# Two chained attention layers on one core: score tiles accumulated as key differences, and each unit's work in a new order

## The reference, cut to what matters

```python
h = group_norm(x)                        # 32 groups, 2 channels each
q, k, v = h @ Wq + bq, h @ Wk + bk, h @ Wv + bv
scores = q @ k.T * 64 ** -0.5            # 1024 x 1024 for each image
o = softmax(scores) @ v
x = x + o @ Wo + bo
```

## Time and profile before

| | |
|---|---|
| median of 3 runs | 185.82 us (185.78 to 186.77) |
| span of the profiled execution, first to last instruction | 184.0 us |
| median less that span (the execution's own time isn't listed apart) | 1.8 us |
| PE busy | 174.6 us (95%) |
| VectorE busy | 138.3 us (75%) |
| GpSimd busy | 121.8 us (66%) |
| ScalarE busy | 100.4 us (55%) |
| chain that ended last | PE 82%, DVE 13% |
| TensorE clock granted | full throughout |

### The profile page before, as it was taken

How to read it: one execution, slowest core, us unless ns; L and a number is a source line. 1 busy time by engine, 2 the same in 40 slices (tenths; PEclk the granted TensorE clock), 3 DMA queues, 4 the chain that set the end, 5 groups by cost and what they waited for, 6 DMA issues and landing times.

```text
span 184.0 us, 3303 instructions
## 1 busy us (share of the span) xinstructions
PE 174.6 (95%) x1223; PEld 93.5 (51%) x1223; DVE 138.3 (75%) x208; ACT 100.4 (55%) x137; POOL 121.8 (66%) x81
## 2 busy tenths in 40 slices
PE   7778899999999999999999999999999999999993
PEld 4435545555525644455535645555535555456661
DVE  2799987779887687859875787769875588386763
ACT  3479367606656376436666476527656554466500
POOL 5265017996799929996699949996799939705000
PEclk9999999999999999999999999999999999999999
DMA  5544100500016000420025000500025100110111
GB/s 154 189 100 98 34 2 0 114 4 2 0 34 142 2 0 14 102 60 0 0 54 122 0 4 20 136 18 0 5 59 115 61 0 21 37 61 7 50 57 57
DMA packets 7103, 8.89 MB, mean 48 GB/s; under 512 B 1656, under 2 KB 4144, under 8 KB 7088
## 3 DMA queue, kind: packets, MB, share of 16 engines
q1 hardware_dynamic: 6080, 7.84, 16.9%
q10 hardware_dynamic: 1008, 0.86, 1.6%
HBM read 1.58 MB, written 1.05 MB: 14 GB/s over the span
## 4 chain that ended last, share of the span: by engine, by line
PE 82%; DVE 13%; DMA 1%; issue 1%; POOL 0%; ACT 0%; DVEq 0%; POOLq 0%
PE ps_attn L887 27%; PE ps_max L817 9%; DVE part_max L588 8%; PE ps_scores L855 8%; PE ps_scores L871 7%; PE ps_scores L857 7%; PE ps_scores L859 7%; PE ps_scores L796 3%; PE ps_misc L804 2%; PE ps_attn L894 2%; PE ps_misc L900 2%; DMA xs<-x_dram 1%; PE ps_misc L894 1%; DVE quarter_rden L628 1%; PE ps_misc L831 1%
## 5 line engine op out<-in xcount | busy, mean ns | idle before, releaser
L313 POOL TENSOR_TENSOR prob_sum<-prob_sum,probs 128x1024 f32<-128x1024 f32 x41 | 97.5, 2377 | 29.0 <-ACT probs L441 16.8
L588 DVE TENSOR_REDUCE part_max<-ps_max 128x2 f32<-128x1024 f32 x60 | 73.4, 1224 | 26.3 <-PE ps_max L818 25.8
L441 ACT ACTIVATE probs<-ps_scores 128x1024 f32<-128x1024 f32 x62 | 61.0, 1025 | 46.1 <-PE ps_scores L872 45.4
L887 PE MATMUL ps_attn<-probs,vals 128*64 128x512 f32 x224 | 54.5, 605 | 0.0
L887 PEld LDWEIGHTS ps_attn<-probs,vals 128*64 128x64 f32 x224 | 13.5, 136 | 27.8 <-issue 19.2
L871 PE MATMUL ps_scores<-q_row,ones_r 64*128 64x512 f32 x62 | 24.5, 396 | 0.5 <-ACT q_row L423 0.5
L872 PE MATMUL ps_scores<-q_row,ones_r 64*128 64x512 f32 x62 | 24.6, 396 | 0.0
L817 PE MATMUL ps_max<-back,front 64*128 64x512 f32 x31 | 13.9, 449 | 2.3 <-DVE part_max L588 1.4
L817 PE MATMUL ps_max<-cross,front 64*128 64x512 f32 x29 | 14.6, 505 | 0.3 <-DVE part_max L588 0.3
L818 PE MATMUL ps_max<-cross,back 64*128 64x512 f32 x29 | 14.6, 505 | 0.0
L818 PE MATMUL ps_max<-front,back 64*128 64x512 f32 x31 | 14.0, 450 | 0.0
(11 more groups left out here) (157 smaller groups left out, 365.7 us busy)
## 6 DMA issues: line engine op xcount, KB each, us to landing
cross<-front SPq DMA_DIRECT2D x16, 128.0 KB, 2.3
cross<-back SPq DMA_DIRECT2D x16, 128.0 KB, 2.3
rden<-quarter_rden SPq DMA_DIRECT2D x44, 32.0 KB, 1.8
xs<-x_dram SPq DMA_DIRECT2D x4, 256.0 KB, 4.6
out_dram<-xs SPq DMA_DIRECT2D x3, 256.0 KB, 2.0
rden<-quarter_rden ACTq DMA_DIRECT2D x12, 32.0 KB, 1.9
q_row<-max_rows SPq DMA_DIRECT2D x14, 2.0 KB
layer<-layers_dram SPq DMA_DIRECT2D x1, 194.5 KB, 2.7
```

The costliest lines, as they stand in the source:

```text
L313: pool.tensor_tensor(total[:, :], total[:, :], probs[t][:, :], ALU.add).then_inc(added, 1)
L441: act.activation(probs[t][:, :], scores_buffer(u, t)[:, :], ACT.Exp, scale=SCALE).then_inc(exp_done, 1)
L588: dve.tensor_reduce(part_max[u % 2][:, at:at + 2 * JS + 1:2 * JS], ps[:, :].rearrange("p (g n) -> p g n", g=2), AX.X, ALU.max, negate=True ...
L887: mm = pe.matmul(ps_attn[half * C:(half + 1) * C, :], v, probs[t][:, cols], start=(t == 0), stop=(t == TILES - 1))
```

## The change

Key tiles are no longer taken one after another with a fresh bank each. Tiles 0 and 1 (key tile 0 of the two halves) are computed as before, with the row of maxima. Tiles 2 to 7 are added onto what the same bank holds after its exponential: the key operand is the difference of two key tiles, so that the sum is the next tile's score with the maximum still in it. The order of key tiles becomes 0, 3, 2, 1.

- `front` and `back` become `query` and `keys`. `keys` has 3 x 512 columns: high parts of all keys for the maxima (HI), and high and low parts of a chain (STEP_HI, STEP_LO): differences of neighbouring key tiles and the last tile (`CHAIN`).
- `project` is four matmuls of 64 rows by 64 columns, into `ps_max` for units from 2 on, instead of two of 64 by 128 into `ps_scores[0]`.
- New: `whole_keys` for every unit (ScalarE, reads the projection), `key_steps` (VectorE, 384 columns), `high_steps` (ScalarE, a unit later) and `low_steps` (VectorE, 512 columns). Gone: `low_back`. `low_front` becomes `low_query`.
- `swap_lo` becomes `swap_steps`, two DMAs of 256 KB, on SyncE behind the rden DMAs; `swap_hi` stands at the window's start.
- In window w all 8 maxima of unit w+1 are computed, in a loop for all w from 0 to 6; M0 also waits for `q_lo` and `k_full`.
- ScalarE: `spread_rden` stands before exp 5, the copies of the projection after exp 7. GpSimd: `root` after add 3; `finish` for units 5 and 6 too, which VectorE did (`finish_tail`).
- The last unit keeps two score buffers; its probs are summed in `late_sum`, the reciprocals are copied in two parts.

The core of the diff:

```diff
-            def low_back(u):
-                dve.wait_ge(back_hi, u)
-                dve.scalar_tensor_tensor(out=back[u % RING][:, LO], in0=ps_scores[0][:, LO],
...
+            def key_steps(u):
+                dve.wait_ge(k_full, u + 1)
+                dve.tensor_tensor(steps[:, HALF:2 * HALF - P], steps[:, 0:HALF - P], steps[:, P:HALF],
+                                  ALU.subtract).then_inc(k_steps, 1)
+            def low_steps(u):
+                dve.wait_ge(steps_hi, u + 1)
+                dve.tensor_tensor(keys[u % RING][:, STEP_LO], steps[:, CHAIN], keys[u % RING][:, STEP_HI].bitcast(F32),
+                                  ALU.subtract).then_inc(steps_lo, 1)
...
             def project(u):
-                pe.matmul(ps_scores[0][:, HI], p[first, 0:P], h[first, :], start=True, stop=True)
-                pe.matmul(ps_scores[0][:, LO], back_w[u // B][second, :], h[second, :], start=True, stop=True).then_inc(proj_mm, 1)
+                ps, top, low = projected(u), slice(0, C), slice(C, P)
+                pe.matmul(ps[top, HI], p[top, WQ:WQ + C], h[top, :], start=True, stop=True)
+                pe.matmul(ps[low, LO], p[top, WK:WK + C], h[top, :], start=True, stop=True)
+                pe.matmul(ps[top, LO], p[low, WK:WK + C], h[low, :], start=True, stop=True)
+                pe.matmul(ps[low, HI], p[low, WQ:WQ + C], h[low, :], start=True, stop=True).then_inc(proj_mm, 1)
...
             def partial_max(u, m, ps=ps_max):
                 if m == 0:
+                    if u >= HEAD:
+                        pe.wait_ge(q_lo, u + 1 - HEAD)
+                        pe.wait_ge(k_full, u + 1)
...
             def scores(u, t):
                 scores_main(u, t)
-                scores_row(u, t)
+                if t < 2:
+                    scores_row(u, t)
...
             def scores_main(u, t):
+                order, n = divmod(t, 2)
+                at = (JS - order) % JS * P
+                key_top, key_low = (own, other) if n else (other, own)
+                pe.matmul(left, key_top[top, hi], q[top, HI], start=t < 2, stop=False, skip_group_check=t >= 2)
...
             for w in range(UNITS):
+                if 0 < w < LAST:
+                    swap_hi(w + 1)
                 if w:
                     spread_rden(w - 1)
-                if w + 2 < UNITS:
-                    swap_hi(w + 2)
-                    swap_lo(w + 2)
+                if 0 < w < LAST - 1:
+                    swap_steps(w + 1)
                 if w + 1 < UNITS:
                     place_rows(w + 1)
...
+            for w in range(LAST):
+                if w:
+                    partial_max(w + 1, 0)
+                    scores(w, 0)
+                scores(w, 1)
+                next_max(1)
+                if w:
+                    values(w - 1, 6)
+                    values(w - 1, 7)
+                next_max(2)
+                scores(w, 2)
+                scores(w, 3)
+                next_max(3)
+                if w:
+                    denominators(w - 1)
+                values(w, 0)
+                next_max(4)
+                scores(w, 4)
+                scores(w, 5)
+                next_max(5)
+                values(w, 1)
+                values(w, 2)
+                next_max(6)
+                scores(w, 6)
+                scores(w, 7)
+                next_max(7)
+                values(w, 3)
+                values(w, 4)
+                turn_max(w + 1)
+                if prep:
+                    project(w + 2)
+                values(w, 5)
+                if prep:
+                    project_v(w + 2)
```

More of the change, by code:

```diff
@@ L203, in scores_buffer, with last_rden, projected @@
         def scores_buffer(unit, t):
-            return ps_scores[t % 2] if unit < LAST else (ps_scores[0], ps_scores[1], ps_max)[t % 3]
+            return ps_scores[t % 2]
+        def last_rden(c):
+            return (ps_max[:, HALF:HALF + HALF // 2], ps_misc[:, HALF // 2:HALF])[c]
+        def projected(unit):
+            return ps_scores[0] if unit < HEAD else ps_max
         block = ctx.enter_context(nc.Block())
@@ L331, in _ @@
             root(1)
-            low_parts(0)
-            low_parts(1)
-            root(2)
+            low_query(0)
+            key_steps(0)
+            low_steps(0)
+            low_query(1)
+            key_steps(1)
+            low_steps(1)
             for w in range(UNITS):
-                if 3 <= w + 2 < UNITS:
-                    root(w + 2)
                 for t in range(2, 2 + pool_adds(w)):
                     add(w, t)
-                    if t == 5 and 0 < w < LAST - 1:
+                    if t == 3 and w + 2 < UNITS:
+                        root(w + 2)
+                    if t == 5 and 0 < w < LAST:
                         finish(w - 1)
+            finish(LAST - 1)
         @block.scalar
@@ L622, in reciprocal @@
                 cols = slice(c * P, (c + 1) * P)
-                sums = ps_misc[:, cols] if u < LAST else ps_max[:, HALF + c * P:HALF + (c + 1) * P]
                 if c == 0:
@@ L760, in _ @@
                 if prep:
-                    low_front(w + 2)
-                    low_back(w + 2)
-                    part(w + 2, 0)
-                    part(w + 2, 1)
-            finish_tail(LAST - 2)
+                    low_query(w + 2)
+                    key_steps(w + 2)
             pair_tail(LAST - 1)
@@ L858, in scores_main @@
[L858 to L860 removed]
+                pe.matmul(left, key_top[top, hi], q[top, HI], start=t < 2, stop=False, skip_group_check=t >= 2)
+                pe.matmul(right, key_low[low, hi], q[low, HI], start=t < 2, stop=False, skip_group_check=t >= 2)
@@ new lines, in scores_main @@
+                pe.matmul(left, key_top[top, hi], q[top, LO], start=False, stop=False, skip_group_check=t >= 2)
+                pe.matmul(right, key_low[low, hi], q[low, LO], start=False, stop=False, skip_group_check=t >= 2)
+                pe.matmul(left, key_top[top, lo], q[top, HI], start=False, stop=t >= 2, skip_group_check=t >= 2)
+                mm = pe.matmul(right, key_low[low, lo], q[low, HI], start=False, stop=t >= 2, skip_group_check=t >= 2)
+                if t >= 2:
+                    mm.then_inc(scores_mm, 1)
```

549 lines of the change are left out of this document (203 added, 346 removed).

## The result

| | before | after |
|---|---|---|
| median, same chip | 186.22 us (4 runs) | 203.03 us (202.15 to 204.27, 4 runs) |
| span of the profiled execution | 184.0 us | 200.9 us |
| TensorE busy | 174.6 us | 173.8 us |
| VectorE busy | 138.3 us | 151.8 us |

The ratio is 1.091 [1.086, 1.096]: the changed kernel is 9% slower. The forecast was 183.7 us (179.3 to 188.2): wrong in sign, and outside its range.

What follows compares the result with a forecast made beforehand. TensorE was taken to set the 20.48 us unit. Head 41.8, five units of 19.9 and tail 40.6 sum to a 181.9 us span; with the median 1.8 above the span, 183.7 us (range 179.3 to 188.2).

Steps and rivals of the forecast that it cites:

- low_steps is new: a 512-column SBUF operation like L667, 0.69 us: VectorE, middle unit, ahead of part6: 0.69 us, some 0.61 of it before the next operation.
- the tail: From the start of window 6 to the span's end: 40.6 us.
- the walk: Step-by-step timing of one new unit from M0 through M7 (next unit's maxima tiles) to the next M0: 19.9 us.
- another page in its place: Skill page TensorEngine Tiling (Array Packing), Restrictions and Gotchas: different row tiles must not write one PSUM bank at once.
- The head: Start of the kernel up to M0 (first maxima tile) of unit 2, put at 41.8 us.
- two swaps of 256 KB land near 21.0: Head: unit 0's step swaps, after low_steps(0) at 17.1, land near 21.0 us; main part at 21.05.
- rival (d): Hand-overs add up: 0.1 us on each of five M waits, unit 20.4, total 186.2 us, no change; chance 0.13.
- rival (b): Project's four quadrants go two and two: 0.9 us in each of 5 units, 6.1 in all, 189.8 us; chance 0.12.
- The worry about two row tiles in one bank: Project: upper and lower rows both write HI's (and LO's) PSUM bank, which a skill page forbids at the same time.
- rival (a): Step swaps or row land late behind six rden issues on SyncE; 1.5 us later gives 187.7 us; chance 0.12.
- The second new wait: Unit's end: next M0 waits until ScalarE's copies and low_query have read project's ps_max; M0 at 19.9, TensorE filled until 19.5.
- rival (c): VectorE's waits are smaller than summed; TensorE keeps the bound at 18.8 to 19.3 a unit, 179.5 us; chance 0.13.

Runs made afterwards that it cites:

- Numbers 1: The kernel before without the row-of-maxima matmul pairs for tiles 2 to 7: 183.16 us, ratio 0.983.
- 12: The kernel after with low_steps on GpSimd, key_steps reading PSUM, high_steps(0) early, and the removed 48 pairs put back as zero-adding pairs: 195.67 us, 1.051.
- numbers 6: The kernel after with low_steps of units 2 to 7 on GpSimd ahead of add 2, run again for a profile: 200.31 us, 1.072.
- number 8: The kernel before with an unused 128 x 512 VectorE sum of two SBUF tiles behind low_back in four units: 191.26 us, 1.025.
- number 5: The kernel after with GpSimd's adds of probs cut from 1024 to 16 columns: 190.34 us, 1.019.
- Numbers 3: The kernel after with VectorE's low_steps moved from between part 5 and part 6 to right behind first_add: 202.22 us, 1.081.
- number 4: The kernel after with six unused matmuls ahead of the first score tile in the head: 200.3 us, 1.076.
- number 9: The kernel after with ScalarE's high_steps(0) put ahead of unit 1's copies in the head: 198.01 us, 1.062.
- number 11: The kernel after with GpSimd's adds cut to 16 columns and high_steps(0) early in the head: 186.91 us, 1.005.

## Why the prediction was wrong

**The bound of the kernel before: right, but too near the next one.** TensorE set the unit, and I wrote that the waits would eat most of its saving (0.6 of 1.7 us left in each unit). Numbers 1 and 12 agree: of 11.0 us of matmuls 3.2 and 4.2 count, and of the 1.38 us in a middle unit 0.2 and 0.4.

**The step that failed: "low_steps is new: a 512-column SBUF operation like L667, 0.69 us".** It took 2.39 us in the mean of six. I took the duration from a row of the right form and size, and didn't ask what GpSimd did beside that row and would do beside the new operation. The trace of before held the answer one line higher. VectorE of the kernel before, in the tail:

```profile
159.56 1.02 DVE L664 TENSOR_TENSOR attn<-attn,rden 128x512 f32<-128x512 f32 x1 [3.87 <-DMA rden<-quarter_rden]
160.62 0.69 DVE L667 TENSOR_TENSOR xs<-attn,xs 128x512 f32<-128x512 f32 x1
```

And its GpSimd:

```profile
152.62 7.41 POOL L313 TENSOR_TENSOR prob_sum<-prob_sum,probs 128x1024 f32<-128x1024 f32 x3
```

GpSimd's adds end at 160.03, and L664 ends 0.55 later, as in numbers 6 and 8 and in the kernel after. L667 behind it runs alone, in 0.69. Two equal instructions, one of 0.69 us and one of 1.02, were the sign to look at. The other VectorE operation on two SBUF tiles, first_add, met no add in the kernel before: all eight take 1.21 to 1.23 us. GpSimd's first add of the same unit waits for its result (8.2 us <-DVE prob_sum L618 in the earlier trace rows), and those of the unit before were over, if barely: the last ends at 106.08, first_add starts at 106.17.

The duration of such an operation is then, by an estimate from these rows, the rest of GpSimd's instruction and most of its own time, between 0.69 and about 0.6 + 2.4 = 3.0 us. What it still needs when GpSimd's instruction ends is 0.14 us less than its own time at each width seen: 0.55 of 0.69, 0.42 of 0.56 for 384 columns, and 1.08 of 1.22 for 1024 (186.79 + 2.46 - 188.17 in the tail of the kernel after). No run says what the 0.14 is. At the walk's place it was 2.52, 1.8 over the price, and all of it lay on VectorE's gapless stretch that sets M7: 16.22 for 14.5. My range had no term for it.

What decides is the operands. VectorE of the kernel after, behind the next project:

```profile
111.63 0.75 DVE L591 SCALAR_TENSOR_TENSOR query<-ps_max,q_bias,query 128x512 fp32r<-128x512 f32 x1 [2.47 <-ACT query L400]
112.78 0.75 DVE L598 TENSOR_TENSOR steps<-steps 128x384 f32<-128x384 f32 x1 [0.40 <-ACT steps L422]
```

And GpSimd:

```profile
110.75 2.37 POOL L328 TENSOR_TENSOR prob_sum<-prob_sum,probs 128x1024 f32<-128x1024 f32 x1
```

Both start inside one add, which ends at 113.12. `low_query` reads PSUM and one SBUF tile and is done in its usual 0.75 us, at 112.38, in the midst of the add. `key_steps` reads two SBUF tiles and ends at 113.53, 0.41 behind the add, 0.2 us longer than when alone (0.56 in number 5).

The Trainium skill's page SBUF — State Buffer, Who interferes with whom, states this rule: VectorE's second SBUF input comes through a read port that it shares with GpSimd, and against a GpSimd instruction that reads SBUF whichever starts first holds the port until it ends. That spoke against this change, and the prediction weighed another page in its place. Numbers 3, 5, 6 and 8 agree with the rule: 0.69 beside an idle GpSimd, 1.84 to 2.52 beside an add; and so do the rows just shown, where an operation with one SBUF input doesn't grow. That the cause is this port rather than something else the two engines share isn't shown by a run.

**How much it cost.** Against number 5, whose VectorE and TensorE do the same work, the stretch from M0 of unit 2 to the start of window 6 takes 111.2 us for 101.8 (148.55 - 46.71): 9.4 us. The tail takes 44.2 for 42.4 (190.9 - 148.55): 1.8. Together 11.2 of the 19.0. Two operations of the tail that grew stand on the chain that ended last, `low_steps` of the last unit and the first late sum, both on VectorE:

```profile
164.62 1.77 DVE L603 TENSOR_TENSOR keys<-steps,keys 128x512 fp32r<-128x512 f32 x1
...
186.79 2.46 DVE L684 TENSOR_TENSOR late_sum<-probs 128x1024 f32<-128x1024 f32 x1 [1.99 <-ACT probs L460]
```

In number 5 they take 0.68 and 1.23 us.

**The head: the landing was mis-sized, and the clock left out.** The chain was right up to the issue: high_steps ends at 15.9 (prediction: 15.8), low_steps at 17.26 (17.1). But I wrote "two swaps of 256 KB land near 21.0" from 2.3 us for 128 KB. The second one's issue took 1.43 us in place of 0.6, a 256 KB swap needs 3.3 to landing, and tile 0 began at 22.10. I also took TensorE's wait as lost time only. It cost the clock as well: 1.7 us by number 4. Together the head is 3.7 us late, and number 9 gets all of it back (41.32; the walk said 41.8).

**The walk itself: 4.1 us short.** In number 5 units take 20.2 to 20.3 us against 19.9. VectorE's part of the walk is right to 0.05 us (M7 at 14.53), and the 0.3 lie behind M7: values start 0.43 us after an f32r pair (107.19 to 107.62) and not 0.31, and from project to M0 are 3.2 us (109.69 to 112.90), not 3.1. Over five units, the last of them longer, that is 101.8 - 99.5 = 2.3 us; the tail is 42.4 and not 40.6, 1.8. This is what rival (d) said, hand-overs that add up, but behind M7 and not on the waits of the M, and number 11 shows that it suffices to take the gain away: 186.91 for 183.7.

**What was right.** Project's four quadrants run beside each other: its second records start 0.48 us behind the first (109.69, 110.17), so rival (b) falls. The worry about two row tiles in one bank falls for this shape too: L776 to L778 start at 109.69 to 109.71, and the scores come out right. The mid-kernel swaps land in time, no score tile of the middle waits on DMA: rival (a) falls there. Its sign, score tile 0 waiting over 0.5 us on DMA, shows in the head, though not for its reason: no rden issues stand before the swap there. The second new wait is there: M0 released by the copy to `steps`, with 0.23 us idle. TensorE waits ahead of M3 to M7 as walked, so rival (c) falls.

**The sum, closed.** 19.0 us over the walk: collisions 11.2, head 3.7, walk 4.1. Measured on medians: without GpSimd's adds 12.7 less, without the head's fault 5.0 less, without both 16.1 less (203.03 - 186.91). 16.1 and the 3.2 to 183.7 make the whole gap of 19.3.

**What stays open.** A version free of collisions that keeps M0 at its early place would be worth what number 11 shows, at most about level. The two savings of 12.7 and 5.0 overlap by 1.6. About 0.7 of the 5.0 is the first unit's shorter collision (number 9), which number 5 removes as well; the rest may be the head's clock, which was less low in number 5's runs, and isn't settled. A second sum of the tail, `prob_sum` with `late_sum` (L670), takes 2.19 us for 1.22 in the kernel after and in number 5 too: it meets GpSimd's `attn` times rden, which that edit leaves. It isn't on the chain that ended last, and no run prices it.

## What to carry to other kernels

Before you place a VectorE operation on two SBUF operands, look at GpSimd's timeline at that moment: price it as the rest of GpSimd's instruction and its own time, and look in the trace for equal instructions whose durations differ, since no wait will show it. Moving it only helps if the next such operation doesn't slide under GpSimd's work in its turn; one operand in PSUM, or a place where GpSimd is known to wait, does. GpSimd is held up in its turn where VectorE's operation starts first. Work taken from an engine whose partner's loop is nearly as long pays by what is left after the partner's waits grow: here a third of it.

## What the runs showed of the hardware

- A VectorE operation on two SBUF tiles that starts inside a GpSimd add ends about 0.4 us (128 x 384), 0.55 us (128 x 512) or 1.1 us (128 x 1024) behind that add. It took up to 2.52 for 0.69 us in the middle of the kernel after, 2.61 for 0.56 in the first unit, and 2.46 for 1.22 (128 x 1024) in the tail. One with an operand in PSUM kept its 0.62 or 0.75 us.
- GpSimd waits as well: its `attn` times rden, started at 99.72 inside number 8's probe, took 1.73 us and not 1.27, and its `low_steps`, started inside `first_add`, 2.12. Both end 1.1 to 1.2 us behind VectorE's operation.
- Four 64 x 64 quadrants of TensorE wrote two PSUM banks beside each other, 0.48 us from group to group.
- A swap of 256 KB between partition halves took 3.3 us to landing, one of 128 KB 2.3 (medians of 16).
- TensorE was idle from 19.6 to 22.1 us, and the granted clock fell to 0.50 (1.2 GHz) near 21.9 and stayed there until 32, a mean of 0.74 in 20 to 40 us. With six matmuls in the gap, or with no gap, it is 1.00.
